# A transformer block on one core: both ends of a hand-written schedule reordered, the last second matmul taken by halves, and products without a result in the tensor queue

## The reference, cut to what matters

```
x = x + attn_block(_ln(x));  x = x + ffn_block(_ln(x))

def attn_block(x):                      # linear attention, then an MLP
    n = layer_norm(x, ln1_w, ln1_b)
    Q = elu(n @ q_w.T + q_b) + 1        # 64 features
    K = elu(n @ k_w.T + k_b) + 1
    V = n @ v_w.T + v_b
    attn = causal(Q K^T) V / (causal(Q K^T) 1 + eps)
    x = x + attn @ o_w.T + o_b
    h = gelu(layer_norm(x, ln2_w, ln2_b) @ f1_w.T + f1_b)      # 1024 wide
    return x + h @ f2_w.T + f2_b

def ffn_block(x):                       # weights made ternary by their mean size
    h = gelu(x @ ternary(W_fc).T)                              # 1024 wide
    return layer_norm(h, ln_w, ln_b) @ ternary(W_proj).T
```

## Time and profile before

| what | value |
|---|---|
| time, median of 3 runs | 489.58 us (488.97 to 490.57) |
| the profiled execution's own time | 487.23 us |
| its span, first to last instruction | 485.5 us |
| mean granted TensorE clock | 0.975 |
| busy: PE, DVE, ACT, POOL | 455.8, 379.1, 326.1, 135.3 us |

### The profile page before, as it was taken

How to read it: one execution, slowest core, us unless ns; L and a number is a source line. 1 busy time by engine, 2 the same in 40 slices (tenths; PEclk the granted TensorE clock), 3 DMA queues, 4 the chain that set the end, 5 groups by cost and what they waited for, 6 DMA issues and landing times.

```text
span 485.5 us, 8738 instructions
## 1 busy us (share of the span) xinstructions
PE 455.8 (94%) x3058; PEld 413.8 (85%) x3058; DVE 379.1 (78%) x995; ACT 326.1 (67%) x611; POOL 135.3 (28%) x132
## 2 busy tenths in 40 slices
...
GB/s 260 120 93 38 1 0 1 45 22 2 1 23 44 23 1 23 45 22 1 2 56 11 23 1 23 45 23 0 2 65 24 1 2 22 2 22 1 24 0 45
DMA packets 10043, 14.08 MB, mean 29 GB/s; under 512 B 784, under 2 KB 9104, under 8 KB 9488
## 3 DMA queue, kind: packets, MB, share of 16 engines
...
...
## 4 chain that ended last, share of the span: by engine, by line
PE 69%; DVE 12%; issue 10%; POOL 3%; ACT 3%; DMA 0%; DVEq 0%; POOLq 0%; ACTq 0%
PE bank_f L367 9%; PE bank_p L397 9%; PE bank_y L178 6%; PE bank_y L179 5%; PE bank_y L180 5%; PE bank_f L178 5%; PE bank_f L179 5%; PE bank_f L180 5%; PE bank_y L381 4%; PE bank_a L178 3%; PE bank_a L180 3%; PE bank_a L179 3%; PE bank_a L186 2%; DVE sh L789 2%; DVE g_lo L933 2%
## 5 line engine op out<-in xcount | busy, mean ns | idle before, releaser
L1036 POOL TENSOR_TENSOR rs<-ve,neg_half 128x2 f32<-128x2 f32 x48 | 33.7, 703 | 196.2 <-DVE ve L784 195.6
L178 PE MATMUL bank_y<-wf_hi,h_hi 128*128 128x256 f32 x256 | 72.1, 282 | 1.0 <-DVE h_lo L811 1.0
L179 PE MATMUL bank_y<-wf_lo,h_hi 128*128 128x256 f32 x256 | 71.5, 279 | 0.0
L180 PE MATMUL bank_y<-wf_hi,h_lo 128*128 128x256 f32 x256 | 71.4, 279 | 0.0
L623 ACT ACTIVATE g_hi<-bank_y,vec 128x256 fp32r<-128x256 f32 x128 | 53.5, 472 | 19.6 <-PE bank_y L381 18.0
L811 DVE TENSOR_TENSOR h_lo<-bank_f,h_hi 128x512 fp32r<-128x512 f32 x64 | 43.9, 688 | 28.3 <-ACT h_hi L593 27.5
L397 PE MATMUL bank_p<-wpj_t,g_hi 128*128 128x256 f32 x256 | 64.9, 289 | 0.2 <-DVE y_yc L942 0.2
L397 PE MATMUL bank_p<-wpj_t,g_lo 128*128 128x256 f32 x256 | 62.6, 279 | 0.0
L933 DVE SCALAR_TENSOR_TENSOR g_lo<-bank_y,vec,g_hi 128x256 fp32r<-128x256 f32 x128 | 55.0, 476 | 5.6 <-ACT g_hi L623 5.0
L367 PE MATMUL bank_f<-wfc_t,z3T_hi 128*128 128x512 f32 x128 | 54.5, 426 | 0.6 <-DVE z3T_lo L811 0.5
L178 PE MATMUL bank_f<-z2T_hi,wf_hi 128*128 128x512 f32 x128 | 52.7, 412 | 1.4 <-DVE z2T_lo L811 1.4
...
## 6 DMA issues: line engine op xcount, KB each, us to landing
...
h<-in_f SPq DMA_DIRECT2D x1, 1024.0 KB, 7.6
y_yc<-in_f SPq DMA_DIRECT2D x1, 1024.0 KB, 9.5
h<-in_fc SPq DMA_DIRECT2D x1, 1024.0 KB, 11.5
h<-in_pj SPq DMA_DIRECT2D x1, 1024.0 KB, 4.7
...
```

What stands on the lines that cost most here:

```text
L178: pe.matmul(ps, w[0], r[0], start=start, stop=False, skip_group_check=skip)
L179: pe.matmul(ps, w[0], r[1], start=False, stop=False, skip_group_check=skip)
L180: return pe.matmul(ps, w[1], r[0], start=False, stop=stop, skip_group_check=skip)
L1036: pool.tensor_tensor(rs[n][:, 2 * h:2 * h + 2], ve[n][:, 2 * h:2 * h + 2], neg_half[:, 0:2], ALU.pow).then_inc(s[f"ln{n + 1}_rs"], 1)
```

## The change

- **Two fronts.** Slice 0 gets banks of its own for its attention (`a_bank`, `v_bank`), there are two buffers for x (`x_two`), the load of slice 1's x goes ahead of those of f2 and fc, and slice 1's norm and transposes move up between those of slice 0. `v_mm(0, h)` waits only for u and the weights and stands before the scores. `f1b` moves behind the attention, the threshold of the ternary weights is made in two parts.
- **Products without a result.** 24 matmuls of 512 columns whose result nobody reads: 11 of zeros at the very start, 8 before and 5 behind `scores(0)`.
- **The last second matmul by halves.** For slice 7, `f2h(7, k, h)` does the two tiles of one half, all of half 0 ends before half 1, and `y_sum` waits for its half alone. The hidden tiles 4 to 7 of slice 7 go to buffers that nothing needs any more (`h_tile`).
- **Order.** The lists `first`, `step` and `last` of all four engines are written anew, those of `step` too.

The diff, cut to its core: of the lists the new lines that the rest speaks of, the old ones are in the functions above; renamed banks and waits that follow from them are left out:

```
+        def x_loaded(g, h):
+
+            return f"{('even', 'odd')[g % 2]}_x_loaded{h}"
+
+        def a_bank(g, i):
+
+            return (bank_a[0], bank_a[1], bank_q)[i] if g else (bank_f[0], bank_f[1], bank_p)[i]
+
+        def v_bank(g, h):
+
+            return bank_a[h] if g else bank_y[h]
+
+        def h_tile(part, g, m):
+
+            if g < G - 1 or m < RH:
+                return hr[part][:, (8 * g + m) % RH, :]
+            return ((uT[0][:, 0, :], uT[0][:, 1, :], uT[1][:, 0, :], uT[1][:, 1, :]),
+                    (q_stack[:], k_stack[:], ad[0][:], ad[1][:]))[part][m - RH]
 
...
-        x_sb = sb("x_sb", [P, T, D])
+        x_two = [sb("x_even", [P, T, D]), sb("x_odd", [P, T, D])]
...
             sp.dma_start(f1_raw, f1_d).then_inc(s["f1_loaded"], 16)
+            load_x(1)
             sp.dma_start(f2_raw, f2_d).then_inc(s["f2_loaded"], 16)
             sp.dma_start(fc_raw, fc_d).then_inc(s["fc_loaded"], 16)
             sp.wait_ge(s["wf1_lo"], 4)
             sp.wait_ge(s["f1b_done"], 1)
             sp.dma_start(pj_raw, pj_d).then_inc(s["pj_loaded"], 16)
-            load_x(1)
...
+            def idle_products(n):
+
+                pe.wait_ge(s["k_lo_cleared"], 1)
+                for _ in range(n):
+                    pe.matmul(bank_q[:], k_lo[:, 0:P], k_lo[:], start=True, stop=True)
+
+            def idle_products_later(n):
+
+                pe.wait_ge(s["bo_ready"], 1)
+                for _ in range(n):
+                    pe.matmul(bank_q[:], wvo[0][:, 0, 0:P], wvo[0][:].rearrange("p k d -> p (k d)"), start=True, stop=True)
...
             def f1b():
                 pe.wait_ge(s["f1_loaded"], 16)
                 pe.wait_ge(s["vec_loaded"], 16)
+                pe.wait_ge(s["v_lo"], 1)
...
             def v_mm(g, h):
-                pe.wait_ge(s["ae_lo" if h == 0 else "af_lo"], g + 1)
-                if g == 0:
+                if g:
+                    pe.wait_ge(s["ae_lo" if h == 0 else "af_lo"], g + 1)
+                else:
+                    pe.wait_ge(s["u_lo"], h + 1)
                     pe.wait_ge(s["wvo_lo"], 2)
...
+            def f2_part(g, k, h):
+                pe.wait_ge(s["h_lo"], 8 * g + k + 1)
+                for t in (2 * h, 2 * h + 1):
+                    mm = split3(bank_y[h][:, (t % 2) * D:(t % 2 + 1) * D],
+                                [h_tile(part, g, k)[:, t * P:(t + 1) * P] for part in range(2)],
+                                [w[:, k, :] for w in wf2], k == 0 and t % 2 == 0, k == KH - 1, skip=True)
+                return mm
...
+            def f2h(g, k, h):
+
+                if k == 0:
+                    pe.wait_ge(s["g_lo"], 16 * (g - 1) + 14 + 2 * h)
+                f2_part(g, k, h).then_inc(s[f"f2_half{h}"], 1)
...
+                idle_products(11); qkb(); wvo_mm(); tu(0, 0); tu(0, 1); bvo(); v_mm(0, 0); qk_mm(0); v_mm(0, 1)
+                idle_products_later(8); scores(0); idle_products_later(5); attend(0, 0); attend(0, 1); attend(0, 2); attend(0, 3); f1b(); tu(1, 0); theta_sum(0); tu(1, 1); tz2(0, 0)
+                tz2(0, 1); qk_mm(1); f1(0, 0); f1(0, 1); theta_sum(1); f1(0, 2); f1(0, 3); f2(0, 0); f2(0, 1)
+                f1(0, 4); f2(0, 2); f1(0, 5); f2(0, 3); cpj(); f1(0, 6); spread(); scores(1); f2(0, 4); f1(0, 7)
+                f2(0, 5); f2(0, 6); f2(0, 7); v_mm(1, 0); v_mm(1, 1); attend(1, 0); attend(1, 1); tz3(0, 0)
+                attend(1, 2); fc(0, 0, 0); tz3(0, 1); attend(1, 3); fc(0, 0, 1); fc(0, 1, 0); fc(0, 1, 1)
+                tr(0, 0, 0); tr(0, 0, 1); fc(0, 2, 0); fc(0, 2, 1); tr(0, 0, 2); proj(0, 0, 0); fc(0, 3, 0)
+                tz2(1, 0); proj(0, 0, 1); tz2(1, 1); tr(0, 0, 3); fc(0, 3, 1); tr(0, 1, 0)
 
...
+                proj(g - 1, 0, 2); tu(g + 1, 0); f1(g, 0); f1(g, 1); proj(g - 1, 0, 3); tr(g - 1, 1, 1)
+                tr(g - 1, 1, 2); tu(g + 1, 1); proj(g - 1, 1, 0); f1(g, 2); tr(g - 1, 1, 3); f1(g, 3); qk_mm(g + 1)
+                f2(g, 0); f2(g, 1); f1(g, 4); f2(g, 2); f1(g, 5); f2(g, 3); f1(g, 6); f1(g, 7); scores(g + 1)
+                f2(g, 4); f2(g, 5); f2(g, 6); f2(g, 7); v_mm(g + 1, 0); proj(g - 1, 1, 1); v_mm(g + 1, 1)
+                proj(g - 1, 1, 2); proj(g - 1, 1, 3); attend(g + 1, 0); tz3(g, 0); attend(g + 1, 1); tz3(g, 1)
+                attend(g + 1, 2); fc(g, 0, 0); attend(g + 1, 3); fc(g, 0, 1); fc(g, 1, 0); fc(g, 1, 1); tr(g, 0, 0)
+                fc(g, 2, 0); tz2(g + 1, 0); fc(g, 2, 1); tr(g, 0, 1); fc(g, 3, 0); tr(g, 0, 2); proj(g, 0, 0)
+                fc(g, 3, 1); proj(g, 0, 1); tr(g, 0, 3); tz2(g + 1, 1); tr(g, 1, 0)
...
+                proj(6, 1, 0); f1(7, 4); f2h(7, 0, 0); tr(6, 1, 3); f1(7, 5); f2h(7, 1, 0); f2h(7, 2, 0)
+                f2h(7, 3, 0); f1(7, 6); f2h(7, 4, 0); f1(7, 7); f2h(7, 5, 0); f2h(7, 0, 1); f2h(7, 6, 0)
+                f2h(7, 1, 1); f2h(7, 7, 0); f2h(7, 2, 1); f2h(7, 3, 1); f2h(7, 4, 1); f2h(7, 5, 1); f2h(7, 6, 1)
+                f2h(7, 7, 1); proj(6, 1, 1); tz3(7, 0); proj(6, 1, 2); proj(6, 1, 3); fc(7, 0, 0); tz3(7, 1)
                 fc(7, 0, 1); fc(7, 1, 0); fc(7, 1, 1); tr(7, 0, 0); fc(7, 2, 0); tr(7, 0, 1); fc(7, 2, 1)
...
-                if 8 * g + m >= RH:
+                if g == G - 1 and m >= RH:
+                    act.wait_ge(s["v_done"], 2 * G)
+                elif 8 * g + m >= RH:
                     act.wait_ge(s["f2_done"], 8 * g + m - RH + 1)
...
+                wqk_hi(); u_norm(0, 0); u_norm(0, 1); ln3_hi(); wvo_hi(); u_hi(0, 0); u_hi(0, 1); n1(0); v_hi(0, 0)
+                wf1_hi(0); qk_exp(0); wf1_hi(1); qk_hi(0); v_hi(0, 1); eps_split(); wf1_hi(2); wf2_hi(0); wf1_hi(3)
+                ae_hi(0); af_hi(0); ad_hi(0); u_norm(1, 0); wf2_hi(1); u_norm(1, 1); wf2_hi(2); abs_part(0)
+                abs_part(1); wf2_hi(3); u_hi(1, 0); z2_norm(0, 0); u_hi(1, 1); z2_norm(0, 1); z2_hi(0, 0)
+                z2_hi(0, 1); abs_part(2); abs_part(3); gelu(0, 0); h_hi(0, 0); gelu(0, 1); h_hi(0, 1); gelu(0, 2)
+                h_hi(0, 2); gelu(0, 3); h_hi(0, 3); qk_exp(1); gelu(0, 4); h_hi(0, 4); gelu(0, 5); qk_hi(1); rows()
+                n1(1); gelu(0, 6); h_hi(0, 5); af_hi(1); h_hi(0, 6); ae_hi(1); spread_copy(); ad_hi(1); gelu(0, 7)
...
             def y_sum(g, h):
 
-                dve.wait_ge(s["f2_done"], 8 * g + 8)
+                if g < G - 1:
+                    dve.wait_ge(s["f2_done"], 8 * g + 8)
+                else:
+                    dve.wait_ge(s[f"f2_half{h}"], 8)
...
+                consts(); ln1_stats(0); qk_bias_add(); ln1_shift(0); wide_cols(); ln3_lo(); wqk_lo(); wvo_lo()
+                u_lo(0, 0); u_lo(0, 1); bo_rows(); qk_max(0); v_lo(0, 0); ln1_stats(1); qk_sum(0); wf1_lo(0)
+                wf1_lo(1); qk_lo(0); ln1_shift(1); v_lo(0, 1); eps_lo(); wf1_lo(2); ad_mask(0); ae_lo(0); af_lo(0)
+                ad_lo(0); wf1_lo(3); attn_out(0, 0); ln2_stats(0, 0); attn_out(0, 1); ln2_stats(0, 1)
+                attn_out(0, 2); ln2_var(0, 0); ln2_stats(0, 2); attn_out(0, 3); ln2_stats(0, 3); ln2_shift(0, 0)
+                ln2_var(0, 1); f1_bias_add(); ln2_shift(0, 1); u_lo(1, 0); threshold(0); u_lo(1, 1); z2_lo(0, 0)
+                z2_lo(0, 1); ternary(0); h_lo(0, 0); qk_max(1); h_lo(0, 1); threshold(1); ternary(1); h_lo(0, 2)
+                ternary(2); h_lo(0, 3); qk_sum(1); ternary(3); h_lo(0, 4); selectors(); qk_lo(1); ln1_stats(2)
...
+                g_lo(g - 1, 0, 3); g_lo(g - 1, 1, 0); output(g - 1, 0); h_lo(g, 0); u_lo(g + 1, 0)
+                g_lo(g - 1, 1, 1); h_lo(g, 1); u_lo(g + 1, 1); g_lo(g - 1, 1, 2); g_lo(g - 1, 1, 3); qk_max(g + 1)
+                h_lo(g, 2); ln4_stats(g - 1, 2); h_lo(g, 3); qk_sum(g + 1); h_lo(g, 4); h_lo(g, 5); qk_lo(g + 1)
+                ln4_stats(g - 1, 3); h_lo(g, 6); ad_mask(g + 1); ln4_var(g - 1, 1); correct(g - 1, 1); h_lo(g, 7)
+                af_lo(g + 1); ad_lo(g + 1); ae_lo(g + 1); y_sum(g, 0); ln3_stats(g, 0); y_sum(g, 1); ln3_stats(g, 1)
+                ln3_shift(g, 0); v_lo(g + 1, 0); ln3_shift(g, 1); output(g - 1, 1); v_lo(g + 1, 1)
+                attn_out(g + 1, 0); z3_lo(g, 0); attn_out(g + 1, 1); ln2_stats(g + 1, 0); ln2_stats(g + 1, 1)
+                z3_lo(g, 1); ln2_var(g + 1, 0); attn_out(g + 1, 2); ln2_stats(g + 1, 2); ln2_shift(g + 1, 0)
+                attn_out(g + 1, 3); ln1_stats(g + 2); ln2_stats(g + 1, 3); ln2_var(g + 1, 1); g_lo(g, 0, 0)
...
+                h_lo(7, 7); correct(6, 1); y_sum(7, 0); ln3_stats(7, 0); ln3_shift(7, 0); y_sum(7, 1)
+                ln3_stats(7, 1); z3_lo(7, 0); ln3_shift(7, 1); output(6, 1); z3_lo(7, 1); ln4_stats(7, 0)
...
+                consts(); ln1_rstd(0); n1o(0); ln1_rstd(1); wf2_lo(0); ln2_rstd(0, 0); ln2_rstd(0, 1); wf2_lo(1)
+                wf2_lo(2); wf2_lo(3); xpb(0); xs(0); ln1_rstd(2); n1o(1); ln3_rstd(0, 0); ln3_rstd(0, 1)
+                ln2_rstd(1, 0); y_cpj(0); ln2_rstd(1, 1); xpb(1); xs(1); ln4_rstd(0, 0)
```

349 lines of the change are left out of this document (156 added, 193 removed).

## The result

The changed kernel takes 493.39 us (median of 12 runs, 491.61 to 495.84), the kernel before 489.05 us in its 12 runs beside it (487.55 to 490.57). The ratio is 1.0092, its 95% interval 1.0073 to 1.0110: 0.9% slower, where I had forecast 1.6% faster. The profiled execution took 492.31 us, its span is 490.5 us and its mean clock 0.982.

The account below looks back on a forecast made before the run. TensorE, busy 455.8 of the 485.5 us span, was taken to bound the kernel. Gains of 2.2 + 0.5 + 1.4 + 3.6 = 7.7 us off the 489.58 us median gave 481.9 us, range 477.5 to 488.

Parts of the forecast that it names:

- The five equal steps: Middle of the kernel: each wait met with 0.2 to 0.6 us to spare, so a gain of 0.
- last end: Behind slice 7's second matmul: halves start fc(7,0,1) 2.6 us sooner, the clock adds 1.0: 3.6 us gained.
- rival (e): Slower: in the middle steps a 1.2 us shift beside POOL delays v_lo and z3_lo; 11 us lost, 492.9 us; chance 0.07.
- Rival (d): Middle steps, reordered, get holes of about 1.4 us that eat the gain: no measurable change, 489 us; chance 0.07.
- front: From the loads to the first gelu: work done ahead wins 2.4 us, less 0.2: 2.2 us gained.
- between (slice 0 to 1): Holes from 60 to 120 us: the 1.6 us wait for a g_lo at 103 about halved; 0.5 us gained.
- 360 to 452 (slice 5 to 7): TensorE idle 1.0 and 1.8 us there, mostly behind g_lo; half of it won: 1.4 us.
- Rival (a): Clock falls again in the new holes behind the last second matmul; price 2.9 us, 484.8 us; chance 0.15.
- Rival (c): At the start: if TensorE begins at the half clock, the eleven products save 3.4 us more, 478.5 us; chance 0.14.
- The eight and five products: Around scores(0), 18.0 to 19.9 and 27.8 to 29.9: end with the work that hides them; without that cover, cost 2.

Follow-up runs that it names:

- old steps: The changed kernel with the step(g) lists of the kernel before on all four engines, its two ends kept: 481.42 us, ratio 0.9836 to the kernel before.
- joint mended: Kernel with the step(g) lists of before, with slice 7's first norm and transposes moved behind slice 6's first gelu and f1: 476.41 us, ratio 0.9757.
- small additions: The changed kernel with POOL's n1o, xpb, xs and y_cpj adds on 2 columns of one tile instead of 512: 473.33 us, ratio 0.9666.

## Why the prediction was wrong

**The step that failed** is "The five equal steps have nothing to win; in my walk each wait in them is met with 0.2 to 0.6 us to spare: 0." A step takes 57.0 us instead of 53.9. I walked the new lists with the durations of the old trace. The 0.48 us of one instruction of `correct` hold only while POOL is idle, and the new lists move POOL's additions beside it (1.24 us in the mean). A margin of 0.2 to 0.6 us is no margin against 2.1 us of stretch in one place. I had the mechanism in the text, for the shift alone: it is in the sum of the last end, where the long shift came as said (1.25 us at 463.74), and in rival (e) at the wrong two places. POOL's list for `step(g)`, old and new, stands in the experiments above; it shows both real ones.

**Rival (e)** is what happened: POOL beside DVE's two-input instructions. It was priced at 2 x 1.1 us in five steps, 11 us, ending at 492.9; the runs show 12.0 us for the new step lists and 493.39. That the two agree so well is partly luck: a step lost 3.1 us and not 2.2, and the old lists have the hole of 2.5 us at the joint, which the new ones don't. Its places were not v_lo and z3_lo but h_lo(g, 7) and g_lo(g, 0, 3), and the instruction that carries most of it is `correct`. The argument against it, that no step of before shows such a hole, was no argument: the old POOL list is what kept `correct` and the additions apart. The old trace does have the stretch in every step, only without a hole behind it: a shift of 1.20 us at 187.63, beside an addition from 187.54 on, and a variance of 1.14 us where 0.17 is usual:

```profile
199.67 1.14 DVE L784 TENSOR_SCALAR ve<-mv 128x2 f32<-128x2 f32 x1
```

I looked for holes, and the sign was in the durations. The rival had 0.07, far too little. Rival (d), holes of 1.4 us a step and no measurable change, had the right size for one of the two holes.

**The terms of the sum.** 7.7 us were forecast for the ends; with the old steps it is 8.4 in the medians and 7.6 in the profiles. That agreement is partly luck, since the terms are off in both directions. By the stretches of the table, with the old steps and, last, with the joint mended as well:

| term | forecast | old steps | joint mended |
|---|---|---|---|
| front | 2.2 | 3.2 | 3.4 |
| between (slice 0 to 1) | 0.5 | 1.7 | 1.8 |
| 360 to 452 (slice 5 to 7) | 1.4 | 0.7 | 3.1 |
| last end | 3.6 | 2.1 | 3.6 |
| sum, with the steps | 7.7 | 7.6 | 11.8 |

- Front: the size can't be had from one trace. `y_sum(0, 0)` stands between 71.37 and 75.76 in the nine profiled kernels with exactly this front, the changed one at 73.13; their median is 72.73, 2.0 us sooner than the 74.75 of the one trace of before. The walk held: scores at 23.30 (24.3 said), attention over at 33.4 (34.0), pj load issued at 37.39 (37.7), qk_mm(1) at 42.15 (42.05), first h_lo ended at 49.23 (48.5), with 0.6 us of wait behind it.
- Between and 360 to 452: in the changed kernel the stretch from slice 5 to 7 won 3.7 us, more than the 1.4, and slice 0 to 1 lost 1.4, since the first collision of `step(1)` lies there. With the old steps the hole at the joint takes 2.5 us out of the stretch from slice 5 to 7.
- Last end: 3.6 in the changed kernel too. fc(7,0,1) starts at 468.24, 7.3 us behind the last part of f2 at 460.9, as said, with the two waits of 1.16 and 1.41 us in place of 1.0 and 1.4. With the old steps the clock took 1.5 us of it.

**Rival (a)**, the clock falling again in those holes, had 0.15 and is not rare: the clock row of the page shows a dip in the last 40 us in 5 of the 12 profiled kernels that have the halves, the changed kernel not among them. In the one with the old steps these two windows show it and its end:

```profile
454.50:460.00 5.50, 5.50 (x21) 4.29 (x21) 2.42 (x6) 2.36 (x5) 0.76 (x1) 0.72 0.00 0
460.00:466.00 6.00, 6.00 (x46) 5.60 (x45) 5.42 (x17) 4.57 (x11) 0.71 (x1) 1.00 0.00 0
```

There the stretch behind the last f2 took 31.05 us instead of 29.59: a price of 1.5 us, half of the 2.9 that I gave it.

**Rival (c)**, and a misreading. I wrote that "the clock is 1.00 from 0 on, and the first real matmuls ran at full speed, wvo_mm 3.42 us". Eleven products of 512 columns in 4.67 us are 0.42 us each, the spacing of the half clock, with the clock column at 1.00 all the while; behind them wvo_mm takes 1.97 us. So 3.42 us was the half clock for most of the way: without the eleven, wvo_mm takes 3.75. Of 12 profiled kernels with the eleven products ten show 1.97, the changed one among them (the two others 3.75 and 3.62). The sign that I had named for this rival, a clock below 1 in the first 6 us, can't appear in that column. The Trainium skill (TensorE: Matmul & The Clock Gate, Part 1) says that the idle default is the half clock; the trace agrees, by these durations, against its own clock column. The mechanism is right and its size small: 1.4 us at the first score, not 3.4, and nothing that the medians resolve. At `y_sum(0, 0)` it is 71.51 against 72.96, which lies within the scatter given above.

**The eight and five products** did not keep the clock up before the attention. In the first of these windows of the changed kernel it is at its lower level; the second shows the same behind the attention, up to the first gelu:

```profile
22.80:29.50 6.70, 6.20 (x23) 5.50 (x23) 6.33 (x11) 5.34 (x11) 1.31 (x1) 0.50 0.00 0
36.65:46.70 10.05, 9.21 (x32) 7.46 (x33) 6.93 (x11) 7.58 (x13) 7.95 (x7) 0.51 0.47 157
```

I had priced them at nothing, and in the medians that is what they cost and bring. The trace without them says that they can still matter: they keep TensorE at work ahead of the attention, and in that one execution without them the attention took about 2 us more.

**What stays open.** Of the 3.1 us that a step loses the two waits are 2.65; the rest isn't on a wait line but in TensorE's busy time, 54.4 us against 53.9. With POOL's old list a step still takes 54.6 us, with small additions 53.63, so POOL's additions cost another 1.0 us; 0.2 of it is a wait, and the rest is again busy time (54.4 against 53.6). What DVE still does there beside the additions is stretched (in a step the shifts take 3.0 us in all instead of 0.9, the variances of 128x2 2.0 instead of 1.0, and one of 128x4 1.34 instead of 0.17), but which of it reaches TensorE I didn't separate. Nor is it shown why the old step lists bear a shift of 1.20 and a variance of 1.14 us in each step without a wait; I take it that they have more slack at those places, but no run measured it.
